# D x U term moved inside the scan loop, the gate read from a kept copy, a stack's first K projection in a PSUM slot of its own, and the last two units' residual made by TensorE

## The chip, the cores and the metric

The kernel runs on one core of one Trainium2 chip. Time is what the device takes for one execution, in microseconds (us); lower is better. A core has five engines with their own instruction streams: PE (TensorE, matrix products), DVE (VectorE), ACT (ScalarE), POOL (GpSimd) and SP, which issues transfers. They wait for one another through semaphores.

## What is computed

Input x is 2048 x 128. A stack of six layers is applied at half weight, then a Mamba block, then the same stack again, each on the layer-normalised x:

```python
x = x + 0.5 * ffn_stack(layernorm(x))
x = x + mamba(layernorm(x))
x = x + 0.5 * ffn_stack(layernorm(x))

# one of the six layers of a stack
x = attn_layer(shift_tokens(x), Wqkv, q_scale, k_scale, Wo) + x
x = ffn_layer(shift_tokens(x), g, b, W1, b1, W2, b2) + x

# attn_layer: 16 heads of 64, a window of 32 with the window before it
q, k, v = split(x @ Wqkv); q, k = l2norm(q) * qs, l2norm(k) * ks
q, k = rotated(q), rotated(k)
out = local_attention(q, k, v) @ Wo

# mamba, after projections, convolution and silu; 256 channels, 16 states
def step(s, inp):
    dA_t, dBu_t, C_t = inp
    s = dA_t * s + dBu_t
    y = einsum('bdn,bn->bd', s, C_t)
y = ys + u * D
y = y * silu(res)
return y @ out_w + x
```

## The kernel before

**Stacks.** `tensor_stack`, `scalar_stack`, `vector_stack` and `pool_stack` are the four engines' programs of a stack; `r` is 0 for the first and 1 for the second. A layer is cut into 16 tiles of 128 tokens, so a stack has N = 96 tiles, and tiles follow one another in a software pipeline: in step `s` an engine does the K projection of tile s - 19, the Q projection of tile s - 18 and so on, in an order written out by hand. PSUM is `PS` with four slots of two banks; `PSB` is the same memory by bank (slot s holds banks 2s and 2s + 1). Slot 0 takes the Q and, after it, the K projection of a tile. For each of these, ACT squares it into `SQ`, DVE multiplies it twice by tables (`q_rotate1`, `q_rotate2`, `k_rotate1`, `k_rotate2`; the second product goes to `T2`, which Q and K share), DVE sums the squares, and POOL adds the halves (`q_add_halves`, L1681, and `k_add_halves`, L1687) and scales them (`q_normalise`, L1695, and `k_normalise`, L1703) by inverse norms that ACT makes from the sums of both. POOL's order at the entry is: add the halves of Q of tile 0, `low_weights` for V (L1663), `low_input` (L1654), add the halves of K of tile 0, then scale Q. `keep_clock` is a few products whose result nobody reads. The feed-forward part works on units of 512 tokens, the last two of a stack on 256 (`UNITS - 2` and `UNITS - 1`): `low_part` (L1715, XNL = what the rounded XNH leaves), the up products, ACT's gelu, DVE's `gate`, the down products (L527), and in the last layer DVE's `half_output` (L1399 and L1401), which adds product, bias and X.

**Scan loop.** Between the stacks the Mamba block scans 2048 tokens in four chunks `h` of 512, and in each chunk 16 states `n`: 64 iterations k = 16 h + n. For each k:

- PE `spread(k + 2)` (L789) copies rows of B and C to all partitions in PSUM slot (k + 2) % 2, and `accumulate(k - 1)` (L708) adds state k - 1's product PR to the sums in banks 6 and 7.
- DVE `drive(k + 1)` multiplies DU by B (L1603 for half of the channels; L1599 for all of them when (k + 1) % 4 is 3), then two scans (L1619) with `input_step` (L1562) between them at k = 8 and 24.
- ACT `decay` (L1208, two per k), `evacuate(k + 1)` (L1194: B and C to SBUF) and `keep_state` (L1202).
- POOL `drive(k + 1)` (L1798, the other half of the channels, not when (k + 1) % 4 is 3) and `read_out(k)` (L1806: PR = state times C).

PE's stream holds `spread(k + 2)` behind `accumulate(k - 2)`, and `accumulate(k - 2)` waits for `read_out(k - 2)`. At n = 0 `accumulate` starts the sums with D times u (L706, matrix `DG`). When a chunk's 16 states are in, DVE's `gate_out` (L1639) reads the sums from PSUM and multiplies them by RES, between the two scans of k % 16 = 1. At k % 16 = 5 PE's `mamba_out` (L808 and L810) projects the gated chunk and then waits until ACT has copied the result into X (L1219, in iteration k % 16 = 6). The fourth chunk is projected inside the second stack's `q_project(1)`.

## Time and profile before

| | |
|---|---|
| Three timed runs | 3346.1, 3350.98 and 3351.53 us; median 3350.98 us |
| The profiled execution | 3348.16 us, of which its span (first to last instruction) is 3346.4 us |
| Busy | PE 3190.6 us (95%), DVE 2794.2 (84%), ACT 2504.1 (75%), POOL 2438.6 (73%) |
| First stack, Mamba block, second stack | from 0, from about 1541 and from about 1810 us of the span |
| Scan loop | from about 1584 to 1810 us |

A busy share is an average over stages. The steady stages of the stacks, in which PE is busy nearly throughout, are not touched by the change; the scan loop, the first two tiles of each stack and the last two units of each stack are.

### The profile page before, as it was taken

How to read it: one execution, taken by the hardware profiler on the slowest of the kernel's cores; microseconds unless marked ns; L12 is line 12 of the kernel's file. 1: busy time of each engine (PE TensorE's matmuls, PEld its weight loads, DVE VectorE, ACT ScalarE, POOL GpSimd, SP SyncE). 2: the span in 40 equal slices, each digit the busy share in tenths (PEclk: the TensorE clock that was granted, in tenths of full speed). 3: DMA queues.
4: the chain of work that ended last, by engine and by line, in shares of the span. 5: the costliest groups of instructions: out<-in, count | busy, mean ns of one | idle time of the engine just before them, and what ended most of it. 6: DMA issues, size and time to landing. Idle time of an engine off the chain costs nothing.

```text
span 3346.4 us, 120438 instructions
## 1 busy us (share of the span) xinstructions
PE 3190.6 (95%) x51618; PEld 2522.9 (75%) x51618; DVE 2794.2 (84%) x3204; ACT 2504.1 (75%) x3163; POOL 2438.6 (73%) x1233
## 2 busy tenths in 40 slices
PE   7999999999999999998888899999999999999999
PEld 5888888887887887874333788888888878788777
DVE  7888888888888888877897888888888888888886
ACT  5777777777777777777675677777777777777776
POOL 6777777777776776763898777777768768768764
PEclk8999999999999999999999999999999999999999
DMA  3333333233233332221000332323323323323322
GB/s 113 89 76 87 75 83 88 68 90 85 67 89 84 73 83 65 71 72 60 1 0 0 86 76 69 93 68 83 91 65 88 88 69 86 91 71 80 74 64 69
DMA packets 142299, 245.22 MB, mean 73 GB/s; under 512 B 32397, under 2 KB 34638, under 8 KB 141774
## 3 DMA queue, kind: packets, MB, share of 16 engines
q1 hardware_dynamic: 141774, 237.51, 27.9%
q8 instruction: 415, 6.80, 0.9%
q14 instruction: 110, 0.90, 0.1%
HBM read 35.01 MB, written 1.05 MB: 11 GB/s over the span
## 4 chain that ended last, share of the span: by engine, by line
PE 39%; issue 4%; DVE 3%; POOL 2%; ACT 2%; DVEq 0%; POOLq 0%; ACTq 0%
PE PS L270 7%; PE PS L390 6%; PE PS L214 4%; PE PS L410 4%; PE PS L216 3%; PE PS L215 3%; PE PS L331 3%; PE PS L527 2%; ACT ARENA L912 1%; DVE ARENA L1619 1%; PE PS L474 1%; PE PS L475 1%; PE PS L476 1%; POOL ARENA L1806 1%; PE PS L433 1%
## 5 line engine op out<-in xcount | busy, mean ns | idle before, releaser
L1695 POOL TENSOR_TENSOR ARENA<-ARENA,RN 128x1024 f32<-128x1024 f32 x192 | 365.4, 1903 | 456.5 <-ACT RN L902 456.5
L270 PE MATMUL PS<-C,ARENA 128*128 128x128 f32 x4608 | 613.5, 276 | 34.4 <-ACT ARENA L912 16.3
L1687 POOL TENSOR_TENSOR ARENA<-ARENA 128x1024 f32<-128x1024 f32 x192 | 468.4, 2439 | 233.9 <-DVE ARENA L1284 233.0
L270 PEld LDWEIGHTS PS<-C,ARENA 128*128 128x128 f32 x4608 | 512.0, 141 | 111.0 <-issue 76.6
L214 PE MATMUL PS<-WL,XH 128*128 128x512 f32 x1152 | 490.0, 425 | 14.0 <-DVE ARENA L1284 7.5
L965 ACT ACTIVATE ARENA<-PS 64x1024 f32<-64x1024 f32 x384 | 390.2, 1016 | 98.0 <-PE PS L270 94.7
L1681 POOL TENSOR_TENSOR ARENA<-ARENA 128x1024 f32<-128x1024 f32 x192 | 458.0, 2385 | 6.5 <-DVE ARENA L1269 6.4
L216 PE MATMUL PS<-WH,XH 128*128 128x512 f32 x1152 | 455.3, 395 | 0.0
L215 PE MATMUL PS<-WH,XL 128*128 128x512 f32 x1152 | 453.4, 394 | 0.0
L390 PE MATMUL PS<-ARENA 128*64 128x64 f32 x12288 | 401.1, 224 | 40.7 <-DVE ARENA L1322 24.5
L390 PEld LDWEIGHTS PS<-ARENA 128*64 128x64 f32 x12288 | 376.1, 138 | 75.8 <-issue 75.8
L1260 DVE TENSOR_TENSOR ARENA<-PS,TAB 128x1024 f32<-128x1024 f32 x192 | 235.2, 1225 | 226.3 <-ACT ARENA L881 226.3
L1709 POOL TENSOR_TENSOR ARENA<-ARENA,RI 128x1024 f32<-128x1024 f32 x192 | 365.7, 1905 | 47.5 <-DVE RI L1333 41.2
L410 PEld LDWEIGHTS PS<-ARENA 128*128 128x128 f32 x3072 | 372.2, 192 | 17.9 <-ACT ARENA L974 1.5
L1703 POOL TENSOR_TENSOR ARENA<-ARENA,RN 128x1024 f32<-128x1024 f32 x192 | 373.8, 1947 | 1.4 <-ACT RN L902 1.4
L410 PE MATMUL PS<-ARENA 128*128 128x128 f32 x3072 | 373.8, 275 | 1.1 <-ACT ARENA L974 1.1
L331 PEld LDWEIGHTS PS<-ARENA 64*32 64x32 f32 x24576 | 292.7, 105 | 69.7 <-issue 59.3
L331 PE MATMUL PS<-ARENA 64*32 64x64 f32 x24576 | 326.3, 223 | 0.2
L1314 DVE TENSOR_REDUCE MX<-PS 128x16 f32<-128x1024 f32 x192 | 234.5, 1221 | 94.6 <-PE PS L331 91.9
L974 ACT ACTIVATE ARENA<-PS 128x1024 f32<-128x1024 f32 x192 | 196.8, 1025 | 137.6 <-PE PS L390 137.6
L881 ACT ACTIVATE ARENA<-PS 128x1024 f32<-128x1024 f32 x192 | 197.2, 1027 | 100.3 <-PE PS L216 100.3
L214 PEld LDWEIGHTS PS<-WL,XH 128*128 128x128 f32 x1152 | 218.2, 189 | 70.9 <-issue 10.7
(155 smaller groups left out, 6493.9 us busy)
## 6 DMA issues: line engine op xcount, KB each, us to landing
ARENA<-ARENA SPq DMA_DIRECT2D x1152, 128.0 KB, 2.4
ARENA<-ARENA SPq DMA_DIRECT2D x768, 64.0 KB, 2.1
ARENA<-in_wqkv SPq DMA_DIRECT2D x36, 512.0 KB, 4.9
ARENA<-in_wo SPq DMA_DIRECT2D x12, 512.0 KB, 3.9
ARENA<-in_w SPq DMA_DIRECT2D x12, 341.0 KB, 4.0
ARENA<-in_w SPq DMA_DIRECT2D x12, 192.0 KB, 3.9
X<-in_xT SPq DMA_DIRECT2D x4, 256.0 KB, 5.0
out<-X SPq DMA_DIRECT2D x1, 768.0 KB, 3.5
```

What stands on the lines that cost most here:

```text
L214: nc.tensor.matmul(o, XH[:, x], WL[:, s], start=True, stop=False)
L215: nc.tensor.matmul(o, XL[:, x], WH[:, s], start=False, stop=False)
L216: last = nc.tensor.matmul(o, XH[:, x], WH[:, s], start=False, stop=True)
L270: last = nc.tensor.transpose(PS[:, slot, 128 * j:128 * j + 128], src[:, 128 * j:128 * j + 128], ident)
L331: last = nc.tensor.matmul(PS[32 * win:32 * win + 32, slot, c:c + 64], q[a:b, hp, 32 * win:32 * win + 32], kt[a:b, hp, 32 * win:32 * win + ...
L390: last = nc.tensor.matmul(out.rearrange("p (a q) -> p a q", a=2)[:, :, col:col + 32], v2[:, win, hp, :], pt[:, hp, win, :], start=True, st ...
L410: last = nc.tensor.matmul(PSB[:, bank, 0:128], w[:, 128 * j:128 * j + 128], OTS[:, 128 * j:128 * j + 128], start=j == 0, stop=j == 7)
L965: last = act.activation(blocks[a:b, :, par, :], PS[a:b, slot, :].rearrange("p (b q) -> p b q", q=32), ACT.Copy)
L1681: nc.gpsimd.tensor_tensor(QN[n % 2], QN[n % 2], T2, ALU.add).then_inc(q_add, 1)
L1687: nc.gpsimd.tensor_tensor(KN[n % 2], KN[n % 2], T2, ALU.add).then_inc(k_add, 1)
L1703: nc.gpsimd.tensor_tensor(a, a, bc(RN[:, n % 2, 16:32], 64), ALU.mult).then_inc(k_nrm, 1)
L1709: nc.gpsimd.tensor_tensor(heads(P), heads(P), bc(RI[:, n % 2, :], 64), ALU.mult).then_inc(p_nrm, 1)
```

## The change

1. **D x u.** It leaves `accumulate` at n = 0, which now starts the sums itself; after `accumulate` at n = 7 two products (new L718) add it.
2. **The gate.** ACT's new `keep_sums` copies the sums from banks 6 and 7 into Y at the end of iteration k % 16 = 1, and PE's next chunk waits for that (`m_yc`). DVE multiplies Y by RES in one instruction (new L1663, two SBUF inputs) between the scans of k % 16 = 4. The fourth chunk is gated from PSUM as before (`gate_last`).
3. **mamba_out** goes from k % 16 = 5 to 9, ACT's copy from 6 to 10.
4. **A stack's entry.** K of tile 0 is projected into slot 1 and no longer waits for `q_rotate2(0)`; its squares go to SB. Q of tile 1 waits for `q_rotate2(0)` and no longer for `k_rotate2(0)`. `carry(0)`, which writes slot 1, waits for `k_rotate2(0)`. DVE's `mamba_residual` of the second stack goes to the place ahead of `q_sums(0)`. The `keep_clock` products at K of tile 0 are gone; those at K of tile 1 are 3 where they were 4.
5. **A stack's last two units.** PE adds X with one more product per unit (`ident` times X), DVE's `half_output` is then one instruction of 128 x 256 where it was two, `low_part` of these units is DVE's, and the down products wait for each `gate` singly.

```diff
         def accumulate(pe, k):
...
                 pe.wait_ge(m_dl, 4)
-                pe.wait_ge(m_dg, 1)
             elif n == 0:
-                pe.wait_ge(m_yd, 2 * h)
+                pe.wait_ge(m_yc, 2 * h)
             for b in range(2):
-                if n == 0:
-                    nc.tensor.matmul(PSB[:, 6 + b, :], DG[:, 128 * b:128 * b + 128], UC[:, h, b, :], start=True, stop=False,
-                                     skip_group_check=True)
-                last = nc.tensor.matmul(PSB[:, 6 + b, :], ident, PR[k % 2][:, b, :], start=False, stop=n == 15,
+                last = nc.tensor.matmul(PSB[:, 6 + b, :], ident, PR[k % 2][:, b, :], start=n == 0, stop=n == 15,
                                         skip_group_check=True)
             last.then_inc(m_y, 1)
+            if n == 7:
+                pe.wait_ge(m_dg, 1)
+                for b in range(2):
+                    nc.tensor.matmul(PSB[:, 6 + b, :], DG[:, 128 * b:128 * b + 128], UC[:, h, b, :], start=False, stop=False,
+                                     skip_group_check=True)
...
-                if 0 <= h < 3 and k % 16 == 5:
+                if 0 <= h < 3 and k % 16 == 9:
                     pe.wait_ge(m_bev, k + 1)
                     mamba_out(pe, h, 2 * (k % 2))
...
+            def keep_sums(h):
+                act.wait_ge(m_y, 16 * h + 16)
+                for b in range(2):
+                    act.activation(Y[:, h, b, :], PSB[:, 6 + b, :], ACT.Copy).then_inc(m_yc, 1)
...
-                if h >= 0 and k % 16 == 1:
-                    gate_out(dve, h)
+                if h >= 0 and k % 16 == 4:
+                    dve.wait_ge(m_yc, 2 * h + 2)
+                    nc.vector.tensor_tensor(Y[:, h, :, :], Y[:, h, :, :], RES[:, h, :, :], ALU.mult).then_inc(m_yg, 1)
                 scan(k, 1)
...
                     mean_in(pe, r, 3)
-                    keep_clock(2)
+                    pe.wait_ge(i_done, 4 * r + 3)
+                    keep_clock(2, 5)
+                    pe.wait_ge(q_rot, n0 + 1)
+                    project(1, 0, 0, q_done)
+                    return
...
-                if n < 2:
-                    keep_clock(4)
+                if n == 1:
+                    keep_clock(3, 5)
...
+                if n == 0:
+                    pe.wait_ge(i_done, 4 * r + 2)
+                    project(0, 1, 1, k_done)
+                    return
...
             def down_products(u, bank):
                 q0, w, x = unit(u)
+                if u >= UNITS - 2:
+                    pe.wait_ge(x_half, 5 * r + u - 4 * (NL - 1) + 1)
+                    nc.tensor.matmul(PSB[:, bank, 0:w], ident, X[:, q0:q0 + w], start=True, stop=False)
...
+                if u >= UNITS - 2:
+                    nc.vector.tensor_scalar(X[:, q0:q0 + w], PSB[:, bank, 0:w], b2, None, ALU.add, ALU.bypass).then_inc(f_done, 1)
+                    return
```

PE's stream in the scan loop, from the first `accumulate` of the second chunk (in iteration k = 17) to `mamba_out` (k = 21), before; L706 is D x u, L708 the other products of `accumulate`, L789 `spread`, L808 and L810 `mamba_out`:

```order
L706 MATMUL PS<-ARENA 128x512
L708 MATMUL PS<-ARENA,C 128x512
L706 MATMUL PS<-ARENA 128x512
L708 MATMUL PS<-ARENA,C 128x512
L789 MATMUL PS<-WH,WL 128x512 x2
L708 MATMUL PS<-ARENA,C 128x512 x2
L789 MATMUL PS<-WH,WL 128x512 x2
L708 MATMUL PS<-ARENA,C 128x512 x2
L789 MATMUL PS<-WH,WL 128x512 x2
L708 MATMUL PS<-ARENA,C 128x512 x2
L808 MATMUL PS<-X,C 128x512
L810 MATMUL PS<-ARENA 128x512 x2
```

and in the changed kernel at k = 23 to 25, with L798 `spread`, L712 `accumulate`, L718 D x u, L817 and L819 `mamba_out`:

```order
L798 MATMUL PS<-WH,WL 128x512 x2
L712 MATMUL PS<-ARENA,C 128x512 x2
L798 MATMUL PS<-WH,WL 128x512 x2
L712 MATMUL PS<-ARENA,C 128x512 x2
L718 MATMUL PS<-ARENA 128x512 x2
L817 MATMUL PS<-X,C 128x512
L819 MATMUL PS<-ARENA 128x512 x2
L798 MATMUL PS<-WH,WL 128x512 x2
L712 MATMUL PS<-ARENA,C 128x512 x2
```

Between D x u and `mamba_out` stood the `accumulate`s of three further states; now D x u stands directly in front of `mamba_out`.

DVE's stream at the gate, before: L1619 a scan, L1639 the gate, L1599 the wide `drive`:

```order
L1619 SCALAR_TENSOR_TENSOR ARENA<-PS,ARENA 128x512
L1639 TENSOR_TENSOR ARENA<-PS,ARENA 128x512 x2
L1619 SCALAR_TENSOR_TENSOR ARENA<-PS,ARENA 128x512
L1599 TENSOR_TENSOR ARENA<-ARENA,PS 128x1024
```

and in the changed kernel, where L1648 is a scan, L1663 the gate, L1632 and L1628 `drive`:

```order
L1632 TENSOR_TENSOR ARENA<-ARENA,PS 128x512
L1648 SCALAR_TENSOR_TENSOR ARENA<-PS,ARENA 128x512
L1663 TENSOR_TENSOR ARENA<-ARENA 128x1024
L1648 SCALAR_TENSOR_TENSOR ARENA<-PS,ARENA 128x512
L1632 TENSOR_TENSOR ARENA<-ARENA,PS 128x512
L1648 SCALAR_TENSOR_TENSOR ARENA<-PS,ARENA 128x512 x2
L1628 TENSOR_TENSOR ARENA<-ARENA,PS 128x1024
```

The gate has one instruction of 1024 columns that reads no PSUM, three iterations later.

PE's stream with its waits at the second stack's entry, before: the `keep_clock` products, K of tile 0 (L214 to L216), `mamba_out`, `mean_in(3)` (L192) and Q of tile 1:

```order
L221 MATMUL PS<-X,C 128x256 x3
L214 MATMUL PS<-WL,XH 128x512 [waits s_q_rot,s_w_lok,s_x_lo]
L215 MATMUL PS<-WH,XL 128x512
L216 MATMUL PS<-WH,XH 128x512
L214 MATMUL PS<-WL,XH 128x512
L215 MATMUL PS<-WH,XL 128x512
L216 MATMUL PS<-WH,XH 128x512
L808 MATMUL PS<-X,C 128x512 [waits s_m_yd,s_m_xs]
L810 MATMUL PS<-ARENA 128x512 x2
L192 MATMUL PS<-X,C 128x512 [waits s_m_done]
L221 MATMUL PS<-X,C 128x256 x2
L214 MATMUL PS<-WL,XH 128x512 [waits s_k_rot,s_q_rot,s_w_loq,s_x_lo]
```

and in the changed kernel:

```order
L214 MATMUL PS<-WL,XH 128x512 [waits s_i_done,s_w_lok,s_x_lo]
L215 MATMUL PS<-WH,XL 128x512
L216 MATMUL PS<-WH,XH 128x512
L214 MATMUL PS<-WL,XH 128x512
L215 MATMUL PS<-WH,XL 128x512
L216 MATMUL PS<-WH,XH 128x512
L817 MATMUL PS<-X,C 128x512 [waits s_m_yg,s_m_xs]
L819 MATMUL PS<-ARENA 128x512 x2
L192 MATMUL PS<-X,C 128x512 [waits s_m_done]
L221 MATMUL PS<-X,C 128x256 [waits s_i_done]
L221 MATMUL PS<-X,C 128x256
L214 MATMUL PS<-WL,XH 128x512 [waits s_q_rot]
```

The `keep_clock` products in front of K of tile 0 are gone, and so are its wait for `q_rot` and the wait of Q of tile 1 for `k_rot`.

## Rows read from the trace of the kernel before

**Rows 1.** The page: the span, and each engine's busy time, share and instructions.

```profile
span 3346.4 us, 120438 instructions
...
PE 3190.6 (95%) x51618; PEld 2522.9 (75%) x51618; DVE 2794.2 (84%) x3204; ACT 2504.1 (75%) x3163; POOL 2438.6 (73%) x1233
```

**Rows 2.** Busy by stretch: length; PE, PEld, DVE, ACT, POOL; clock, DMA.

```profile
1645.00:1703.20 58.20, 48.01 (x108) 17.90 (x107) 53.72 (x52) 39.68 (x66) 53.18 (x29) 0.97 0.00 1
1703.20:1760.00 56.80, 47.12 (x109) 17.58 (x107) 51.87 (x51) 40.38 (x66) 52.79 (x30) 1.00 0.00 1
```

**Rows 3.** Groups by line, 1584 to 1810 us: busy, mean ns, idle before, releasers.

```profile
L1806 POOL TENSOR_TENSOR ARENA<-ARENA 128x1024 f32<-128x1024 f32 x63 | 149.9, 2390 | 19.6 <-DVE ARENA L1619 16.8 <-PE PS L708 2.8
...
L1798 POOL TENSOR_TENSOR ARENA<-ARENA 128x512 f32<-128x512 f32 x48 | 63.8, 1329 | 0.9 <-ACT ARENA L1194 0.9
```

**Rows 4.** Timeline, second chunk: start, length, engine, line, tiles, count [idle before <- releaser].

```profile
1646.22 1.29 DVE L1639 TENSOR_TENSOR ARENA<-PS,ARENA 128x512 f32<-128x512 f32 x2 [0.57 <-PE PS L708]
...
1652.56 2.37 POOL L1806 TENSOR_TENSOR ARENA<-ARENA 128x1024 f32<-128x1024 f32 x1 [1.32 <-DVE ARENA L1619]
...
1660.35 1.02 PE L808 MATMUL PS<-X,C 128*128 128x512 f32 x2
...
1664.54 1.22 DVE L1599 TENSOR_TENSOR ARENA<-ARENA,PS 128x1024 f32<-128x1024 f32 x1 [3.27 <-PE PS L789]
...
1668.26 2.36 POOL L1806 TENSOR_TENSOR ARENA<-ARENA 128x1024 f32<-128x1024 f32 x1 [2.70 <-DVE ARENA L1619]
```

**Rows 5.** Timeline around DVE's two `input_step`s (L1562).

```profile
1612.90 3.70 DVE L1562 TENSOR_TENSOR ARENA<-ARENA 128x1024 f32<-128x1024 f32 x1
...
1617.87 2.35 POOL L1806 TENSOR_TENSOR ARENA<-ARENA 128x1024 f32<-128x1024 f32 x1 [2.35 <-DVE ARENA L1619]
...
1672.76 2.49 DVE L1562 TENSOR_TENSOR ARENA<-ARENA 128x1024 f32<-128x1024 f32 x1
...
1674.10 2.28 POOL L1798 TENSOR_TENSOR ARENA<-ARENA 128x512 f32<-128x512 f32 x1
```

**Rows 6.** Timeline of the first chunk: its first accumulate, and 35 us on.

```profile
1589.14 2.07 PE L706 MATMUL PS<-ARENA 128*128 128x512 f32 x2 [2.46 <-POOL ARENA L1806]
...
1595.91 0.69 DVE L1603 TENSOR_TENSOR ARENA<-ARENA,PS 128x512 f32<-128x512 f32 x1 [2.88 <-PE PS L789]
...
1624.17 3.78 PE L708 MATMUL PS<-ARENA,C 128*128 128x512 f32 x4
...
1628.74 0.69 DVE L1603 TENSOR_TENSOR ARENA<-ARENA,PS 128x512 f32<-128x512 f32 x1 [1.40 <-PE PS L789]
```

**Rows 7.** Timeline of the second stack's entry.

```profile
1825.56 3.31 PE L221 MATMUL PS<-X,C 128*128 128x256 f32 x8 [2.51 <-DVE ARENA L1240]
...
1827.97 2.37 POOL L1681 TENSOR_TENSOR ARENA<-ARENA 128x1024 f32<-128x1024 f32 x1 [1.89 <-DVE ARENA L1269]
...
1832.25 1.27 POOL L1654 TENSOR_TENSOR XL<-ARENA,XH 128x512 fp32r<-128x512 f32 x1
...
1833.83 1.22 DVE L1284 TENSOR_TENSOR ARENA<-PS,TAB 128x1024 f32<-128x1024 f32 x1
...
1835.13 2.39 POOL L1687 TENSOR_TENSOR ARENA<-ARENA 128x1024 f32<-128x1024 f32 x1 [1.61 <-DVE ARENA L1284]
...
1838.95 1.90 POOL L1695 TENSOR_TENSOR ARENA<-ARENA,RN 128x1024 f32<-128x1024 f32 x1 [1.43 <-ACT RN L902]
```

**Rows 8.** Timeline of the first stack's entry, POOL.

```profile
30.02 2.38 POOL L1687 TENSOR_TENSOR ARENA<-ARENA 128x1024 f32<-128x1024 f32 x1
...
33.74 1.90 POOL L1695 TENSOR_TENSOR ARENA<-ARENA,RN 128x1024 f32<-128x1024 f32 x1 [1.34 <-ACT RN L902]
```

**Rows 9.** Timeline of the second stack's end.

```profile
3337.01 0.72 POOL L1715 TENSOR_TENSOR XNL<-ARENA,XNH 128x256 fp32r<-128x256 f32 x1 [5.95 <-ACT XNH L1009]
...
3340.17 2.83 PE L527 MATMUL PS<-ARENA 128*128 128x256 f32 x12
...
3343.53 0.49 DVE L1401 SCALAR_TENSOR_TENSOR X<-PS,LP,X 64x256 f32<-64x256 f32 x1
```

More of the change, by code:

```diff
@@ L175, in build @@
             "dt", "min", "ex", "sp", "dl", "du"))
-        m_bc, m_bev, m_cs, m_pr, m_dg, m_y, m_yd, m_out, m_done = (sem("m_" + n) for n in (
-            "bc", "bev", "cs", "pr", "dg", "y", "yd", "out", "done"))
+        m_bc, m_bev, m_cs, m_pr, m_dg, m_y, m_yc, m_yg, m_out, m_done = (sem("m_" + n) for n in (
+            "bc", "bev", "cs", "pr", "dg", "y", "yc", "yg", "out", "done"))
         m_da, m_db, m_sc = ([sem(f"m_{n}{b}") for b in range(2)] for n in ("da", "db", "sc"))
@@ L217, in project, with keep_clock @@
                 last.then_inc(done, 1)
-            def keep_clock(k, bank=3):
+            def keep_clock(k, bank):
                 for _ in range(k):
@@ L312, in carry @@
                     pe.wait_ge(pad_set, r + 1)
+                    pe.wait_ge(k_rot, n0 + 1)
                 s = n + 19
@@ L652, in finish_tiles @@
                 down_products(u + 1, 5)
-                for j in range(3):
-                    units(f_h[j], u + 2)
                 units(f_xm, u + 2)
@@ L878, in q_square @@
                 act.wait_ge(q_done, n0 + n + 1)
-                if n:
+                if n == 1:
+                    act.wait_ge(q_ss, n0 + 1)
+                elif n:
                     act.wait_ge(k_ss, n0 + n)
@@ L889, in k_square @@
                 act.wait_ge(k_done, n0 + n + 1)
-                act.wait_ge(q_ss, n0 + n + 1)
-                act.activation(SQ, PS[:, 0, :], ACT.Square).then_inc(k_sq, 1)
+                if n:
+                    act.wait_ge(q_ss, n0 + n + 1)
+                act.activation(SQ if n else SB, PS[:, 0 if n else 1, :], ACT.Square).then_inc(k_sq, 1)
             def inverse_norms(n):
@@ L1215, in scalar_mamba @@
                 decay(k, 0)
-                if k > 16 and k % 16 == 6:
+                if k > 16 and k % 16 == 10:
                     h = k // 16 - 1
@@ L1224, in scalar_mamba @@
                     evacuate(k + 1)
+                if k > 1 and k % 16 == 1:
+                    keep_sums(k // 16 - 1)
         def layer_tables(l, g):
@@ L1277, in k_rotate1 @@
                     dve.wait_ge(kT_done, n0 + n - 1)
-                nc.vector.tensor_tensor(halves(KN[n % 2]), halves(PS[:, 0, :]), table(n, 2), ALU.mult)
+                nc.vector.tensor_tensor(halves(KN[n % 2]), halves(PS[:, 0 if n else 1, :]), table(n, 2), ALU.mult)
             def k_rotate2(n):
@@ L1283, in k_rotate2 @@
                 dve.wait_ge(q_add, n0 + n + 1)
-                nc.vector.tensor_tensor(halves(T2), halves(PS[:, 0, :])[:, :, ::-1, :], table(n, 3),
+                nc.vector.tensor_tensor(halves(T2), halves(PS[:, 0 if n else 1, :])[:, :, ::-1, :], table(n, 3),
                                         ALU.mult).then_inc(k_rot, 1)
@@ L1292, in q_sums @@
                     return
+                if n == 0 and r == 1:
+                    mamba_residual(dve, 3, 7)
                 dve.wait_ge(q_sq, n0 + n + 1)
@@ L1391, in gate2, with low_part @@
                     gate(x // 4, 2, 2 * 1)
+            def low_part(u):
+                q0, w, x = unit(u)
+                dve.wait_ge(f_hi, c0 + u + 1)
+                nc.vector.tensor_tensor(XNL[:, x], XCT[:, x], XNH[:, x].bitcast(F32), ALU.subtract).then_inc(f_lo, 1)
             def half_output(u, bank):
@@ L1438, in vector_stack @@
             for s in range(114):
-                if s == 18 + 1 and r == 1:
-                    mamba_residual(dve, 3, 7)
                 if s == 18 + 2:
@@ L1487, in vector_stack @@
             normalise(u + 1, 4)
+            low_part(u + 1)
             if r == 0:
@@ L1493, in vector_stack @@
             normalise(u + 2, 4)
+            low_part(u + 2)
             if r == 0:
@@ L1728, in pool_stack @@
             if r == 1:
-                pool.wait_ge(m_yd, 8)
+                pool.wait_ge(m_yg, 4)
                 pool.wait_ge(m_out, 3)
@@ L1760, in pool_stack @@
             p_normalise(95)
-            low_part(UNITS - 2)
             if r == 0:
-                squares(pool, 0)
-                squares(pool, 1)
-            low_part(UNITS - 1)
-            if r == 0:
-                squares(pool, 2)
+                for c in range(3):
+                    squares(pool, c)
         def squares(pool, c):
```

26 lines of the change are left out of this document (12 added, 14 removed).

## The prediction

> **What bounds the kernel now.** I read the page first: PE is busy 95% of a span of 3346.4 us [rows 1]. The change leaves the steady stages alone, so this share says nothing of it, and I read three places instead: the scan loop, the entries and the ends of the stacks. Whatever one of them gains or loses moves everything behind it, since stack, Mamba block and stack follow one another.
>
> In the scan loop I took busy time from gate to gate. The third chunk (1703.2 to 1760) lasts 56.8 us, of which POOL is busy 52.8 and DVE 51.9; PE (47.1) and ACT (40.4) have room [rows 2]. POOL and DVE are thus both nearly full, and the loop's length is POOL's work plus the 4.0 us in which it stands still. The groups say for whom: `read_out` (L1806) waited 16.8 us for DVE's scans and once, 2.8 us, for PE [rows 3]. The timeline shows what makes DVE late, twice in a chunk: the gate (1.29 us, after 0.57 of waiting for PE), which POOL feels as 1.32, and `mamba_out`, for which DVE waits 3.27 and POOL then 2.70 [rows 4]. These two make the 4.0. `mamba_out` costs so much because the next `spread` is queued behind it and behind ACT's copy, and DVE's `drive` waits for that `spread`.
>
> **The scan loop, part by part.**
>
> *D x u out of the first accumulate.* At 1589 PE runs at the lower of its two clocks: one product of D x u takes 2.07 us, and DVE's `drive` waits 2.88 for what stands behind [rows 6]. Without the two products (some 3.4 us there, the second one meeting a rising clock) the next `spread` comes earlier by about 2.1 net of what remains cold. Take -2.1 (bounds 0 and -2.9).
>
> *The clock after k = 8.* DVE's `input_step` there holds everything, PE falls idle and comes back slow: the four passes of an `accumulate` take 3.78 us, and DVE loses 1.40 to it [rows 6]. D x u now lies in just this gap. Take -1.4 (bounds 0 and -1.4).
>
> *D x u in front of mamba_out.* A product of its shape is two passes, 1.02 us at the full clock with the next one starting a little before its end [rows 4]; the two cost 1.8. PE's stream is now `accumulate`, D x u, `mamba_out`, wait for the copy, `spread`, and DVE's wait grows from 3.27 to some 5.1. Before, D x u stood at n = 0, where DVE was at its gate. Nothing covers it now in the third and fourth chunk: +1.8 each. In the second chunk `input_step` (k = 24, 2.49 us on DVE [rows 5]) falls on the same place: before, DVE lost 1.86 + 3.27 + 2.49; now it loses 2.49 for the gate, 2.49 for `input_step`, and 5.1 less the 2.49 by which it is late itself. Both sums are 7.6, so 0. Bounds per chunk: 0, if DVE has gained enough lead since the gate, and +1.8.
>
> *The gate from SBUF.* No such gate is in the trace, but `input_step` has its shape and its kinds of operands. It took 2.49 and 3.70 us, far more than the 1.29 of the gate from PSUM. Both times POOL was working: at 1672.76 DVE got its turn when one POOL instruction ended, and POOL's next one then took 2.28 where its mean is 1.33; at 1612.90 DVE came later still, and POOL idled 2.35 afterwards [rows 3, 5]. POOL has no pause at k % 16 = 4 either. With 2.49 the gate costs DVE 2.49 where it was 1.86 with its wait, +0.6, and POOL's books (held 0.95, then idle some 0.8, where it idled 1.32) say +0.4; take +0.5 per chunk, +1.5. Bounds per chunk: -0.8 (an idle POOL, 1.1 us) and +1.8 (3.70).
>
> The Trainium skill says of this pair ("SBUF — State Buffer", "SBUF: two separate sides") that DVE with two SBUF inputs and a GpSimd op that reads SBUF exclude each other, and that the first to start has the shared ports for its whole instruction. By that rule the gate waits for one POOL instruction and the sum stands as above; by the row of 3.70, in which two POOL instructions passed, it would be 3.7 higher. The rule speaks against moving the gate to SBUF at all.
>
> *keep_sums* costs ACT two copies of 512 columns per chunk, about 1.2 us; ACT is idle 18.5 us of the second chunk [rows 2], the next `decay` is late by a microsecond that DVE spends on the second scan and on `drive`. PE's next chunk waited for DVE's gate at this point and now waits for ACT, no later. Zero; if ACT had no room, +1.2 per chunk.
>
> *The clock at the new gate.* PE is starved there about as at `input_step`. One fall costs up to 1.40 [rows 6]; I put +0.5 for the three.
>
> Loop: -2.1 - 1.4 + 0 + 1.8 + 1.8 + 1.5 + 0.5 = **+2.1**.
>
> **The entries.** In the second stack PE waits 2.51 us, runs the `keep_clock` products, and K of tile 0 comes only after Q's rotation; DVE's `k_rotate2(0)` starts at 1833.83 [rows 7]. With K in its own slot it waits for POOL's Q addition only (1827.97 + 2.37 = 1830.3, [rows 7]), 3.5 earlier. Then POOL binds: `low_weights` and `low_input` (1832.25 + 1.27 = 1833.5) stand ahead of the K addition, so that moves from 1835.13 to 1833.5, ends at 1835.9, and Q's scaling follows it directly instead of at 1838.95: **-3.1** [rows 7]. DVE's `mamba_residual`, now ahead of `q_sums(0)`, holds DVE for less than that. In the first stack POOL's K addition already follows its predecessor without a gap (30.02 to 32.40), so only the wait behind it goes: Q's scaling at 32.4 instead of 33.74 [rows 8], -1.4, and a little more for K of tile 1, which POOL's idle time leaves room for; take **-2.0**. `carry(0)` waits longer but is needed only for the first scores, several steps on. Bounds: 0, if a later wait of the ramp takes it back, and -3.5 and -2.4. Together -5.1.
>
> **The ends.** PE is the chain there: twelve passes of the down products in 2.83 us, 0.236 each, straight behind the up products, then `half_output` with 0.49 for each of its halves [rows 9]. Two products more are four passes, +0.94. One DVE instruction less gives back about 0.5. `low_part` goes from POOL's 0.72 to at most DVE's 0.49 (the nearest row of 256 columns), -0.25 [rows 9]; in the first stack PE waits for DVE's gates instead, so this gain is lost. +0.2 and +0.4, **+0.6**. Bounds 0 and +1.5.
>
> **Sum.** +2.1 - 5.1 + 0.6 = -2.4 us. The profiled execution took 3348.16 us, so 3345.8; from the median of the three timed runs, 3350.98, it is 3348.6. I predict 3347, between the two: no change that can be told, since a measurement of this kernel can tell about 0.2%, 6.7 us.
>
> **Rivals.**
>
> *The loop gains instead (22%).* DVE's lead over POOL, rebuilt between k % 16 = 4 and 9, hides D x u (0 in place of +3.6), and the gate meets POOL's pauses (-0.8 in place of +0.5, three times): -2.4 - 3.6 - 3.9 = -9.9; with half of that, about 3341. For it: PE has 9 us of room in a chunk. Against it: DVE and POOL differ by only 0.9 us of busy time per chunk [rows 2], so no lead grows in five iterations.
>
> *The entries' gain isn't kept (12%).* The ramp has its own waits, and PE's clock may fall in other places of it. Then +2.7: about 3352.
>
> *The gate lets two POOL instructions pass (8%),* as at 1612.90: +1.3 three times, about 3351.
>
> *PE's clock stays low after the new gate: slower (8%).* At that clock an `accumulate` takes 3.78 us [rows 6], and with its `spread`, some 1 us at that clock, more than the 3.55 of an iteration (56.8 / 16), so PE becomes the bound and loses 1.3 us in each of the five iterations up to D x u and `mamba_out`, and these 4 us themselves grow by up to 4: 8 per chunk and +24 in all, about 3370. It decides for slower once each fall costs over 3 us; the fall in the trace cost 1.40, and PE caught up [rows 6].
>
> The forecast itself has 50%. **Range** 3337 to 3356: down to the first rival's better half, up over the second and third with the bounds of the gate. Faster by over 0.2%: 0.26 (the first rival and the lower edge of the forecast); slower: 0.11 (the last rival and the sum of dear gate and lost entries); the same: 0.63.
>
> **What would show it.** Right: POOL's first wait of 2.8 us and DVE's 2.88 gone; full clock at 1620 to 1628; the third and fourth chunks about 2.3 us longer, with DVE waiting 5 us behind `mamba_out` and a gate of about 2.5 us; Q's scaling of tile 0 3 us closer to the end of the scan; last `half_output` at the same distance from the last up product plus a few tenths. Wrong: DVE's wait behind `mamba_out` still 3.3 (D x u hidden), gates of 1.1 or 3.7, or the ramp's later tiles at the old distance.

## The result, and the profile after

The changed kernel takes 3358.01 us (median of 17 runs, 3351.88 to 3359.57), the kernel before 3348.64 in the same comparison (17 runs, 3344.45 to 3351.74). The ratio is 1.0025, with a 95% interval of 1.0018 to 1.0031: slower by 8.4 us (6.0 to 10.4); the medians themselves lie 9.4 apart. The forecast was 3347, with a range up to 3356, and "slower" had a chance of 0.11. It was wrong.

The page of the changed kernel (engine: busy us, share, instructions; then PE's granted clock in 40 slices) answers to [rows 1]:

```profile
span 3355.8 us, 120407 instructions
PE 3199.4 (95%) x51606; PEld 2524.8 (75%) x51606; DVE 2799.7 (83%) x3201; ACT 2506.6 (75%) x3169; POOL 2437.3 (73%) x1229
...
PEclk8999999999999999998999999999999999999999
```

PE is busy 8.8 us longer with 12 products fewer on record, so some of its work ran slower. To find the place I laid both timelines over each other, taking the start of the same DVE instruction in each tile (after less before, in us; the profiled executions):

| place | after less before | so this stretch gave |
|---|---|---|
| first stack, tile 1 / tile 4 | -2.7 / -0.3 | entry: gain there, then lost in the ramp |
| first stack, last tile | -2.0 | a step of -1.5 at tile 86 |
| first scan of the loop begins | -1.8 | end of the first stack: +0.2 |
| last scan of the loop ends | +10.6 | **scan loop: +12.4** (forecast +2.1) |
| second stack, tiles 4 to 20 | +6.7 | entry: -4.0 (forecast -3.1) |
| second stack, tiles 24 to 84 | +8.4 | a step of +1.6 at tile 22 |
| second stack, last tile | +9.5 | a step of +1.2 at tile 86 |
| end of the span | +9.4 | end of the second stack: 0 |

The loop thus carries the whole loss. Its groups by line in the changed kernel (busy us, mean ns, idle time before and who ended it) answer to [rows 3]:

```profile
L1832 POOL TENSOR_TENSOR ARENA<-ARENA 128x1024 f32<-128x1024 f32 x63 | 149.3, 2381 | 28.4 <-DVE ARENA L1648 25.1 <-PE PS L712 3.0
L1632 DVE TENSOR_TENSOR ARENA<-ARENA,PS 128x512 f32<-128x512 f32 x47 | 31.4, 668 | 12.5 <-PE PS L798 12.4
L1628 DVE TENSOR_TENSOR ARENA<-ARENA,PS 128x1024 f32<-128x1024 f32 x16 | 19.5, 1222 | 13.6 <-PE PS L798 11.6 <-DVE ARENA L1648 0.5
L1663 DVE TENSOR_TENSOR ARENA<-ARENA 128x1024 f32<-128x1024 f32 x3 | 10.9, 3642 | 0.0
```

L1832 is `read_out`, L1632 and L1628 are DVE's `drive`, L1648 is the scan, L1663 the gate. POOL waits 25.1 us for DVE's scans where it waited 16.8 [rows 3]; a gate takes 3.64 us where 2.49 was forecast. The timeline at the first gate (start, us, engine, line; in brackets idle time and who ended it) shows what the gate does to the others; it answers to [rows 4]:

```profile
1651.10 2.44 POOL L1832 TENSOR_TENSOR ARENA<-ARENA 128x1024 f32<-128x1024 f32 x1
1652.20 3.65 DVE L1663 TENSOR_TENSOR ARENA<-ARENA 128x1024 f32<-128x1024 f32 x1
1653.40 1.37 POOL L1824 TENSOR_TENSOR ARENA<-ARENA 128x512 f32<-128x512 f32 x1
1655.52 0.72 PE L798 MATMUL PS<-WH,WL 64*128 64x512 f32 x2
1655.77 1.27 DVE L1648 TENSOR_TENSOR_SCAN ARENA<-PS,ARENA 128x512 f32<-128x512 f32 x1
1657.18 2.34 POOL L1832 TENSOR_TENSOR ARENA<-ARENA 128x1024 f32<-128x1024 f32 x1 [2.41 <-DVE ARENA L1648]
1659.57 3.78 PE L712 MATMUL PS<-ARENA,C 128*128 128x512 f32 x4 [3.33 <-POOL ARENA L1832]
1663.28 1.22 PE L798 MATMUL PS<-WH,WL 64*128 64x512 f32 x2
1664.43 3.78 PE L712 MATMUL PS<-ARENA,C 128*128 128x512 f32 x4
1664.54 0.69 DVE L1632 TENSOR_TENSOR ARENA<-ARENA,PS 128x512 f32<-128x512 f32 x1 [0.83 <-PE PS L798]
1669.15 0.69 DVE L1632 TENSOR_TENSOR ARENA<-ARENA,PS 128x512 f32<-128x512 f32 x1 [1.55 <-PE PS L798]
```

Read it from the top. The gate begins while POOL's `read_out` runs, and it ends 1.08 us after POOL's *next* instruction (`drive`, L1824) has ended at 1654.77: two POOL instructions passed. POOL then has nothing for 2.41 us, and PE, which needs POOL's products, stands idle for 3.33. When it goes on, an `accumulate` of four passes takes 3.78 us for 1.98, and DVE waits 0.83 and 1.55 us for the `spread` behind it. The windows of PE there (stretch, length, busy, granted clock) say why:

```profile
1650.00:1655.00 5.00, 4.34 (x12) 1.00 0.00 0
1655.00:1660.00 5.00, 1.67 (x5) 0.84 0.00 0
1660.00:1665.00 5.00, 5.00 (x7) 0.50 0.00 0
1665.00:1670.00 5.00, 5.00 (x8) 0.63 0.00 0
1670.00:1680.00 10.00, 9.31 (x23) 1.00 0.01 2
```

The granted clock of 0.50 is the lower of the two levels, 1.2 GHz. It fell at 1658.42, while PE stood idle, and rose at 1668.66. It looks the same at all three gates: 3.65, 3.63 and 3.64 us, then waits of DVE of 0.83 and 1.55, 0.83 and 1.58, 0.83 and 1.60. Of the rest of the loop, the wait of DVE behind D x u and `mamba_out`:

```profile
1673.43 1.88 PE L718 MATMUL PS<-ARENA 128*128 128x512 f32 x4
1673.47 2.36 POOL L1832 TENSOR_TENSOR ARENA<-ARENA 128x1024 f32<-128x1024 f32 x1 [0.20 <-DVE ARENA L1648]
1673.83 2.45 DVE L1648 TENSOR_TENSOR_SCAN ARENA<-PS,ARENA 128x512 f32<-128x512 f32 x2
1675.14 1.02 PE L817 MATMUL PS<-X,C 128*128 128x512 f32 x2
...
1676.00 1.88 PE L819 MATMUL PS<-ARENA 128*128 128x512 f32 x4
...
1678.57 0.73 PE L798 MATMUL PS<-WH,WL 64*128 64x512 f32 x2 [0.69 <-ACT X L1236]
...
1679.34 1.22 DVE L1628 TENSOR_TENSOR ARENA<-ARENA,PS 128x1024 f32<-128x1024 f32 x1 [3.05 <-PE PS L798]
```

It is 3.05 us here and 4.19 and 4.18 in the next two chunks, for 3.27 before [rows 4].

### The profile page after: what moved, and what is told of

It reads as the page before. It is cut to its first block and busy times, and to the rows that moved or that the text cites. A ratio compares the mean times of both kernels' runs of the same rounds, so it can differ in the third digit from the quotient of the medians.

```text
span 3355.8 us, 120407 instructions
## 1 busy us (share of the span) xinstructions
PE 3199.4 (95%) x51606; PEld 2524.8 (75%) x51606; DVE 2799.7 (83%) x3201; ACT 2506.6 (75%) x3169; POOL 2437.3 (73%) x1229
## 5 line engine op out<-in xcount | busy, mean ns | idle before, releaser
L214 PE MATMUL PS<-WL,XH 128*128 128x512 f32 x1152 | 489.8, 425 | 17.1 <-DVE ARENA L1303 6.2
L216 PE MATMUL PS<-WH,XH 128*128 128x512 f32 x1152 | 456.4, 396 | 0.0
L214 PEld LDWEIGHTS PS<-WL,XH 128*128 128x128 f32 x1152 | 218.7, 190 | 73.9 <-issue 14.2
```

Of the source, the lines that this page charges most:

```text
L214: nc.tensor.matmul(o, XH[:, x], WL[:, s], start=True, stop=False)
L216: last = nc.tensor.matmul(o, XH[:, x], WH[:, s], start=False, stop=True)
```

## The experiments

Each time stands beside runs of the kernel before on the same chip, and the ratio is to those. The kernel before took 3350.01 us beside e1, e3, e5 and e6, 3348.20 beside e2, e4, e8 and e9, and 3350.68 beside e7, e10, e11 and e12, so two medians of different groups compare to some 2 us only. The last column is the time in the profiled execution from the loop's first scan to the end of its last.

| run | what differs from the changed kernel | median us | ratio, 95% | loop us |
|---|---|---|---|---|
| (before) | | 3348.64 | 1 | 225.7 |
| (after) | | 3358.01 | 1.0025, 1.0018 to 1.0031 | 238.1 |
| e1_loop_before | loop as before | 3346.14 | 0.9993, 0.9984 to 1.0001 | 226.8 |
| e7_entries_only | loop and ends as before | 3347.70 | 0.9992, 0.9983 to 1.0001 | 224.2 |
| e3_gate_at_6 | gate at k % 16 = 6 | 3352.91 | 1.0011, 1.0002 to 1.0020 | 233.8 |
| e5_mamba_out_at_5 | `mamba_out` after 5 | 3345.06 | 0.9989, 0.9980 to 0.9998 | 225.6 |
| e6_psum_gate_dxu7_out5 | gate from PSUM, `mamba_out` after 5 | 3346.50 | 0.9993, 0.9984 to 1.0002 | 225.0 |
| e2_psum_gate_out9 | gate from PSUM | 3348.72 | 1.0001, 0.9993 to 1.0010 | 226.7 |
| e9_dxu_first | D x u in front, as before | 3349.87 | 1.0002, 0.9993 to 1.0010 | 227.7 |
| e4_filler_at_gate | surplus products on PE | 3361.83 | 1.0035, 1.0021 to 1.0048 | 241.4 |
| e12_dxu_in_hole | D x u at the gate's step | 3349.48 | 0.9999, 0.9990 to 1.0008 | 227.5 |
| e8_out5_w1_early | `mamba_out` after 5, `w1_low` earlier | 3324.26 | 0.9931, 0.9919 to 0.9944 | 224.7 |
| e10_psum_gate_w1_early | as e6, `w1_low` earlier | 3326.88 | 0.9932, 0.9919 to 0.9944 | 225.8 |
| e11_before_w1_early | kernel before, `w1_low` earlier | 3330.38 | 0.9943, 0.9930 to 0.9955 | 225.8 |

### Is it the loop?

**e1_loop_before** puts the loop back and leaves entries and ends changed.

```diff
-                if h >= 0 and k % 16 == 4:
-                    dve.wait_ge(m_yc, 2 * h + 2)
-                    nc.vector.tensor_tensor(Y[:, h, :, :], Y[:, h, :, :], RES[:, h, :, :], ALU.mult).then_inc(m_yg, 1)
+                if h >= 0 and k % 16 == 1:
+                    dve.wait_ge(m_y, 16 * h + 16)
+                    for b in range(2):
+                        last = nc.vector.tensor_tensor(Y[:, h, b, :], PSB[:, 6 + b, :], RES[:, h, b, :], ALU.mult)
+                    last.then_inc(m_yg, 1)
...
-                if 0 <= h < 3 and k % 16 == 9:
+                if 0 <= h < 3 and k % 16 == 5:
```

(`keep_sums` goes, ACT's copy moves from 10 to 6, and D x u back to n = 0.)

> Scan loop as before (gate from PSUM at k%16=1, D*u in front of a chunk's first sums, mamba_out after k%16=5), entries and ends as changed. Theory (the loss is the loop's: its last scan ended 12.4 us later against its first in the trace of after, entries and ends gained some 3 to 5): 3358.0 - 12.4 = 3345.6, range 3344 to 3348. Rival (the gains at the entries hang on the loop's new ending, or the loss is in the steady units): the time stays above the kernel before's, 3350 to 3354, and the offset in the second stack's tiles 4 to 20 is not 4 us below that at the loop's end.

3346.14, and a loop of 226.8 us for 238.1. The loss is the loop's; the rival falls.

**e7_entries_only** puts the ends back too (X added by DVE, low part made by POOL).

> Both stacks' entries as changed, loop and ends as before. Theory (the ends cost 0.2 and 0.4 by the forecast, which the traces of after bore out at about +0.4 and 0): against the run with the loop as before (3346.1) 0 to 0.6 less: 3345.5, range 3343 to 3348, not to be told from it by the median; in the trace the first scan starts 0.4 earlier against the first stack's last tile. Rival (the ends gain): 3348 to 3350.

3347.70, not to be told from e1. In the traces the stretch from the first stack's last tile to the first scan is 0.4 us (e7) and 0.2 us (e11) longer than in the kernel before, with the same end; with the new end it is 0.2 to 1.7 longer in eleven traces, 1.0 in the mean. That leaves some 0.7 for the first stack's end where 0.4 was forecast, a price that no median shows.

### Gate, place of mamba_out, D x u

**e3_gate_at_6**: one number in DVE's loop.

```diff
-                if h >= 0 and k % 16 == 4:
+                if h >= 0 and k % 16 == 6:
```

> As changed, but the gate stands at k%16=6, where POOL has one multiply to do (the read out) and not two. Theory (two POOL multiplies pass a gate that stands where POOL has two queued, and the stall of 3.33 us that this gives PE lowers its clock): each gate takes 2.5 us or less and not 3.65, PE's idle time there is 2.2 us or less, the clock stays full, and 1.15 + 0.83 + 1.57 = 3.5 us are saved per gate, 10.6 in all: 3347.5, range 3345 to 3351. Rival (the loss is D*u directly in front of mamba_out, which stays): 3354 to 3358. Rival (a gate of any length over some 2.2 us costs the clock): the gate is 2.5 us but the two accumulates after it still take 3.78: 3358 - 3.5 = 3354.5.

3352.91, between the theories. At k % 16 = 6 POOL has only its `read_out`, the gate takes 2.86, 2.84 and 2.85 us, and one POOL instruction passes. But PE still stands idle for 2.12 us at each, and behind two of the three its clock sinks, if later; the passes here come to 2.80 us:

```profile
1663.74 2.35 POOL L1832 TENSOR_TENSOR ARENA<-ARENA 128x1024 f32<-128x1024 f32 x1 [2.41 <-DVE ARENA L1648]
1666.15 2.80 PE L712 MATMUL PS<-ARENA,C 128*128 128x512 f32 x4 [2.12 <-POOL ARENA L1832]
```

Behind `mamba_out` DVE then waits 4.85, 6.93 and 4.97 us. So a gate let past one POOL instruction alone isn't the cure.

**e5_mamba_out_at_5**: the number of `mamba_out` and of ACT's copy.

```diff
-                if 0 <= h < 3 and k % 16 == 9:
+                if 0 <= h < 3 and k % 16 == 5:
...
-                if k > 16 and k % 16 == 10:
+                if k > 16 and k % 16 == 6:
```

> As changed, but mamba_out stands after k%16=5 (its copy at 6) and not 9, so that D*u is not directly in front of it. Theory (the larger part is the gate, its two POOL multiplies and the low clock after it, 3.5 us each): only the wait behind D*u and mamba_out falls away, 3 x 1.8 = 5.4 us: 3352.6, range 3350 to 3355; gates stay at 3.65. But mamba_out then falls in PE's stretch at the low clock, which may cost all of it again: 3357 to 3360. Rival (the loss is at mamba_out alone): 3346 to 3348.

3345.06, 13 us less (12 by the ratios), more than either theory gave: the gate isn't shorter, and yet nothing of the loss is left. Its timeline, in the same places as above:

```profile
1653.53 3.66 DVE L1663 TENSOR_TENSOR ARENA<-ARENA 128x1024 f32<-128x1024 f32 x1
1654.94 1.98 PE L712 MATMUL PS<-ARENA,C 128*128 128x512 f32 x4 [0.68 <-POOL ARENA L1832]
1657.34 1.10 PE L817 MATMUL PS<-X,C 128*128 128x512 f32 x2 [0.42 <-DVE ARENA L1663]
1658.27 1.88 PE L819 MATMUL PS<-ARENA 128*128 128x512 f32 x4
1658.52 2.35 POOL L1832 TENSOR_TENSOR ARENA<-ARENA 128x1024 f32<-128x1024 f32 x1 [2.41 <-DVE ARENA L1648]
1661.45 0.73 PE L798 MATMUL PS<-WH,WL 64*128 64x512 f32 x2 [1.30 <-ACT X L1236]
1662.11 1.98 PE L712 MATMUL PS<-ARENA,C 128*128 128x512 f32 x4
1662.21 1.22 DVE L1628 TENSOR_TENSOR ARENA<-ARENA,PS 128x1024 f32<-128x1024 f32 x1 [0.88 <-PE PS L798]
```

`mamba_out` (L817, L819) now does its 2.8 us of work in the very stretch in which PE stood idle. The `accumulate` behind it takes 1.98, and DVE waits 0.88 for the `spread` where it waited 3 to 4. Two losses go at once: the low clock, and `mamba_out`'s wait, which now falls into the gate's. D x u, now by itself, costs DVE a wait of 1.64 and 1.65 us in the third and fourth chunks.

**e6_psum_gate_dxu7_out5** and **e2_psum_gate_out9** take the SBUF gate away (the first part of e1's diff), and leave D x u in the middle of a chunk.

> As changed, but the gate reads PSUM at k%16=1 and mamba_out stands after k%16=5, as before; of the loop's changes only D*u in the middle of a chunk (k%16=8) is left. Theory (D*u in the middle costs nothing where nothing else of PE's stands beside it, and frees 1.8 to 2.2 us of the first sums of each chunk): 3345.6 of the loop as before, less 2.1 + 1.4 for the first chunk and up to 1.8 for each other: 3342, range 3339 to 3345. Rival (D*u costs its 1.9 us wherever it stands, since PE is the bound in steady steps): 3345 to 3348, that is the same as with the loop as before.

> As changed, but the gate reads PSUM at k%16=1 as before; D*u stays in the middle of a chunk and mamba_out after k%16=9, next behind it. With the run that had mamba_out after 5 (3346.5) this gives the price of the late place alone, without a stall at the gate and without a low clock. Theory (a wait of DVE and POOL for the spread that stands behind D*u and mamba_out in PE's queue, 3.05 to 4.2 us, of which before had 2 already): 3 x 1.8 to 3 x 2.2, thus 3351.9 to 3353.1, range 3350 to 3354. Rival (the place costs nothing if the gate does not disturb): 3346 to 3348. Rival (it carries the whole loss): 3357.

3346.50 and 3348.72. For e6 that is the rival's number, not the theory's 3342: D x u in the middle isn't told from D x u in front (3346.14). Nor is e2 the 3351.9 to 3353.1 expected: the medians lie 2.2 us apart and the intervals overlap; the loops lie 1.7 us apart in the traces, of which 0.8 arises in the first chunk, before any `mamba_out`. DVE's waits in the third chunk say why, first in e6 (behind `mamba_out`, then behind D x u), then in e2 (behind both):

```profile
1720.40 1.22 DVE L1626 TENSOR_TENSOR ARENA<-ARENA,PS 128x1024 f32<-128x1024 f32 x1 [3.26 <-PE PS L798]
1734.48 1.22 DVE L1626 TENSOR_TENSOR ARENA<-ARENA,PS 128x1024 f32<-128x1024 f32 x1 [1.64 <-PE PS L798]
```

```profile
1734.61 1.22 DVE L1626 TENSOR_TENSOR ARENA<-ARENA,PS 128x1024 f32<-128x1024 f32 x1 [4.90 <-PE PS L798]
```

Apart or together, it is 4.90 us. D x u in the middle costs about 1.6 us of waiting in each of these chunks, and its nearness to `mamba_out` adds nothing to that. Against the kernel before, whose D x u stands beside DVE's gate, e2's third and fourth chunks are 1.7 us longer each, which is the +1.8 of the prediction; its first chunk gives 1.9 back and its second 0.5. So without the SBUF gate the changed order costs next to nothing in all.

**e9_dxu_first** keeps gate and place, and takes D x u back in front.

> As changed (gate from SBUF at k%16=4, mamba_out after 9), but D*u stands in front of a chunk's first sums as before, not in the middle. Theory (D*u next to mamba_out costs about 1.8 per chunk and the first chunk's gain was 2.1 to 2.2, the rest of the loss stays with the gate): 3358 - 5.4 + 2.2 + up to 1.4 for the clock after k=8, 3355 to 3356, range 3353 to 3358. Rival (nearness of D*u and mamba_out is the main loss): 3350 or less.

3349.87. That is the rival's number, but not for its reason, since e2 against e6 shows no price of that nearness. The gate itself changed:

```profile
1655.95 2.36 POOL L1831 TENSOR_TENSOR ARENA<-ARENA 128x1024 f32<-128x1024 f32 x1
1657.50 1.88 DVE L1662 TENSOR_TENSOR ARENA<-ARENA 128x1024 f32<-128x1024 f32 x1
1658.25 2.26 POOL L1823 TENSOR_TENSOR ARENA<-ARENA 128x512 f32<-128x512 f32 x1
```

It begins later in POOL's `read_out`, 1.55 us behind its start and not 1.10, gets its turn when that ends, and takes 1.88 or 1.89 us in each chunk; now POOL's `drive` takes 2.26 for 1.3. The order changed together with a shift of half a microsecond. PE is idle for 2.11 us here, and its clock falls behind two of the three gates, for 3.4 us each and not 10.2. So this edit changed several terms at once and separates none.

### Is it the clock?

**e4_filler_at_gate** was to keep PE busy during the gate.

```diff
+                if k > 16 and k % 16 == 5:
+                    pe.wait_ge(m_bev, k + 2)
+                    for _ in range(8):
+                        one = SEL[64:128, 0:1].broadcast_to([64, 128])
+                        nc.tensor.matmul(PSB[:, 2 * ((k + 1) % 2), :], one, HR[64:128, 0:512], start=True, stop=True)
```

> As changed, with 8 extra products of TensorE in the step of each gate, in the stretch in which it stood idle for 3.33 us (their sums are overwritten; they are surplus work). Theory (of the loop's loss the low clock after the gate is a part of its own: accumulate 3.78 for 1.98, DVE waits 0.83 and 1.57 for the spread behind it): the clock stays full, both waits go, 2.4 us per gate and 7.2 in all: 3350.8, range 3348 to 3353; gates stay at 3.65. Rival (the low clock is hidden behind POOL and DVE, and the loss is mamba_out's place alone): 3356 to 3359.

3361.83, and no test of the theory. The loop is 3.3 us longer still in the trace; the medians' intervals overlap (1.0018 to 1.0031 and 1.0021 to 1.0048). The products waited for ACT, which ended only at 1660.50.

```profile
1657.16 0.73 PE L798 MATMUL PS<-WH,WL 64*128 64x512 f32 x2
1660.50 3.78 PE L815 MATMUL PS<-WH,WL 64*128 64x512 f32 x8 [2.61 <-ACT ARENA L1211]
1664.21 3.78 PE L712 MATMUL PS<-ARENA,C 128*128 128x512 f32 x4
```

PE had been idle for 2.61 us, and the surplus itself ran at the low clock (0.50 from 1660.5 to 1664.3), in front of the work.

**e12_dxu_in_hole** does it with work that is needed and waits for nothing: D x u.

```diff
+            if n == 4:
+                pe.wait_ge(m_dg, 1)
+                for b in range(2):
+                    nc.tensor.matmul(PSB[:, 6 + b, :], DG[:, 128 * b:128 * b + 128], UC[:, h, b, :], start=False, stop=False,
+                                     skip_group_check=True)
             pe.wait_ge(m_pr, k + 1)
...
-            if n == 7:
```

> As changed (gate from SBUF at k%16=4, mamba_out after 9), but D*u's four products stand ahead of PE's wait in front of the accumulate of k%16=4, in the stretch in which PE stood idle for 3.33 us during the gate. The filler of an earlier run came too late for this (it waited for ACT and ran after the clock had fallen); these wait for nothing. Theory (the loop's loss is the low clock that follows PE's idle time at the gate, and needs it): idle time 1.5 us, clock full, accumulates of 1.98, gates still 3.65; 2.4 us per gate for the clock and 0.7 for mamba_out no longer next to D*u (2.2 in three, from the runs with mamba_out after 5 and after 9): 3358.0 - 9.3 = 3348.7, range 3345 to 3351. Rival (the gate's length itself, not PE's clock, holds the loss): at most the 2.2 comes back, 3355.8 or more.

3349.48, 0.8 from the number expected. The three gates still take 3.65, 3.65 and 3.62 us, and the loop is 10.7 us shorter:

```profile
1652.82 3.65 DVE L1663 TENSOR_TENSOR ARENA<-ARENA 128x1024 f32<-128x1024 f32 x1
1656.79 1.98 PE L709 MATMUL PS<-ARENA 128*128 128x512 f32 x4
1657.80 2.35 POOL L1832 TENSOR_TENSOR ARENA<-ARENA 128x1024 f32<-128x1024 f32 x1 [2.41 <-DVE ARENA L1648]
1660.20 1.99 PE L717 MATMUL PS<-ARENA,C 128*128 128x512 f32 x4 [1.43 <-POOL ARENA L1832]
```

POOL stands still for the same 2.41 us as in the changed kernel, PE for 1.43 in place of 3.33; the granted clock is 1.00 in every window from 1640 to 1680, and the waits of 0.83 and 1.55 are gone. `accumulate` goes on 7.38 us behind the gate's start, as in the changed kernel (7.37), so PE's delay at the gate is the same and only its speed behind it differs. Of the 10.7 us, 7.2 are these waits of DVE at three gates: the clock's part. Another 2.7 go with D x u, which no longer stands in front of `mamba_out`: DVE waits 0.88, 3.26 and 3.26 us there for 3.05, 4.19 and 4.18, while `input_step` (k = 24) takes 2.48 for 1.20. The other 0.8 I can't assign. In time the run is 8.5 us faster (8.7 by the ratios), so the clock's part there is some 6, an estimate from these shares.

### The step at tile 22

In each of the changed kernels so far the second stack loses 1.4 us at tile 22. There DVE subtracts W1's high part from W1 (`w1_low`, in `ffn_residual`), reading and writing SBUF alone. In the kernel before, and then in the changed one:

```profile
2142.99 0.90 DVE L1245 TENSOR_TENSOR W1L<-ARENA,W1H 128x682 fp32r<-128x682 f32 x1
2143.13 3.00 POOL L1681 TENSOR_TENSOR ARENA<-ARENA 128x1024 f32<-128x1024 f32 x1
```

```profile
2149.59 2.38 POOL L1712 TENSOR_TENSOR ARENA<-ARENA 128x1024 f32<-128x1024 f32 x1
2149.74 2.95 DVE L1264 TENSOR_TENSOR W1L<-ARENA,W1H 128x682 fp32r<-128x682 f32 x1
```

Before, DVE was first by 0.14 us; now it is second by 0.15 and waits. In all other layers but each stack's first, this subtraction took 2.77 to 2.96 us in both kernels (1.68 in each stack's first). DVE stands idle for 1.02 us a little earlier, waiting for PE's down products, while POOL has not begun. **e8_out5_w1_early** (on e5), **e10_psum_gate_w1_early** (on e6) and **e11_before_w1_early** (on the kernel before) move it there.

```diff
+                if c % 4 == 3:
+                    w1_low(l + 1)
                 par = LP[:, l * NP:(l + 1) * NP]
                 dve.wait_ge(f_y, c0 + c + 1)
...
                 if c % 4 == 3:
-                    w1_low(l + 1)
```

> As the run with SBUF gate and mamba_out after 5 (3345.1), and DVE takes W1's low part in front of a unit's two output adds, not behind them: there DVE stood idle for 1.02 us and POOL's multiply of SBUF had not begun. In the traces this 0.90 us subtraction took 2.96 in 5 of 6 layers of each stack where it began 0.15 us after a POOL multiply, and in the second stack of before, where it began 0.14 us ahead of one, 0.90; that one case is the step of 1.4 us by which all changed kernels lose part of the entry's gain at the 22nd tile. Theory (DVE waits until POOL's multiply is done, and PE stood idle 1.30 behind it): 0.90 to 1.0 each and 1.4 us less per layer, 10 times: 3331, range 3328 to 3336. Rival (the loss is only moved, since the subtraction now delays POOL's multiply or the adds): 3343 to 3347. Rival (the step at tile 22 is something else): the offset in the second stack keeps its step.

> The run with the gate from PSUM, D*u in the middle and mamba_out after 5 (3346.5), with W1's low part ahead of the two output adds. Theory: the same gain as with the SBUF gate (3345.1 to 3324.3, 20.8): 3325.7, range 3323 to 3328.

> The kernel before with the one move of W1's low part, nothing else. Theory (the gain is independent of this change): 3348.5 - 20.8 = 3327.7; less 1.4 because one of before's ten subtractions was short already, so 3329, range 3326 to 3332. Rival (the 20.8 hangs together with the new loop and entries): over 3335.

3324.26, 3326.88 and 3330.38. The 12 subtractions of e8 take 12.1 us where the changed kernel's take 32.6, and its span is 19.4 us shorter than e5's; the step at tile 22 is gone. By the ratios the move is worth 19.4 us on e5, 20.4 on e6 and 19.1 on the kernel before: it does not need this change. The first number is 7 us better than expected: I had counted 1.4 per layer, and the offsets show 1.6 to 1.8 gained in most layers and more in a stack's last (2.4 and 3.9). There a fall of PE's clock ahead of tile 86 is gone too, which 14 of the 22 stacks without the move have and none of the six with it. e8's place, in its own timeline:

```profile
2124.65 0.87 DVE L1264 TENSOR_TENSOR W1L<-ARENA,W1H 128x682 fp32r<-128x682 f32 x1
2125.25 2.03 POOL L1727 TENSOR_TENSOR ARENA<-ARENA,RN 128x1024 f32<-128x1024 f32 x1 [6.52 <-ACT RN L914]
2125.72 0.74 DVE L1445 SCALAR_TENSOR_TENSOR ARENA<-PS,LP,ARENA 64x512 f32<-64x512 f32 x1 [0.19 <-PE PS L541]
```

The output add begins with a wait of 0.19 in place of 1.02: the subtraction fills time in which DVE waited. e8 is faster than both kernels, by 0.69% against the one before.

## Why the prediction was wrong

*Right.* The clock after k = 8 stayed at the full level, as said. It did in all eight traces with D x u behind n = 7, and fell in four of the six without (not in e1 and e11), so this term was a fall that comes in part of the executions only. The end of the second stack: +0.2 forecast, 0 measured.

*The first chunk.* -3.5 forecast in two terms, -1.6 measured at k = 17. D x u out of the first `accumulate` had gained 2.2 by the third `read_out`, the -2.1 forecast, but the loop did not keep it: PE's low clock, which before ended 9.7 us into the loop, now lasted 14.5 us, DVE waited 1.09 and 1.90 at 1592 and 1597, and by k = 4 the loop stood at +0.2. In five other traces with D x u moved the low clock lasted 13.5 to 14.2 us and the gain went in the same way. In e3, e6 and e8 it ended after 7.8, and 2.7 were kept. The clock after k = 8 then gave 1.5. Another 1.0 was luck: `input_step` took 2.67 us for 3.70, which was in no term. By k = 17 1.1 were lost again.

*The second stack's entry.* -3.1 forecast, -4.0 here, and between -2.9 and -6.0 by tile 4 in the eleven other traces with this entry. It looks right and isn't shown. The trace of e11, which has the entry of before, gains 4.6 us over the same stretch against the trace of before: that one has 17 us of low clock between the end of the scan and tile 5, e11 only 3.4. So the execution that I measured against was a slow one in this place. What can be seen of the term itself is that Q's scaling of tile 0 stands 26.6 us behind the last scan's end, for 29.0 before and 28.0 in e11: 2.4 or 1.4 us, not 3.1.

*The first stack's entry.* -2.0 forecast. Tile 1 came 2.7 earlier, and by tile 4 only 0.3 was left; over the twelve traces of kernels with this entry it is 1.0 in the mean against tile 0 (between -3.1 and +0.2), where e11 with the old entry has +0.9. The rival "the ramp takes it back" thus holds for half of the gain against the trace of before, and hardly against that of e11. What in the ramp takes it was not tried. For both entries together, -5.1 forecast, e1 and e7 give 2.3 and 2.7 us by their ratios, with intervals that just reach no change.

*The gate's price.* The step that failed first: "with 2.49 the gate costs DVE 2.49". Of the two rows of `input_step` [rows 5] I took the cheap one as the forecast and gave the dear one 8%. All three gates were of the dear kind, 3.65, 3.63 and 3.64, together +5.7 against before's gates with their waits (1.86, 1.69 and 1.66), where the sum had +1.5. The Trainium skill's rule ("SBUF — State Buffer", "SBUF: two separate sides"), by which I had supported the choice, gives a wait for one POOL instruction, the one that started first. This trace does not agree: the gate's row starts at 1652.20, POOL's `drive` at 1653.40, and yet `drive` too ends before the gate does.

*The clock at the gate.* The step that carries most of it: "+0.5 for the three". In the trace it is 0.83 + 1.55 at the first gate and as much at the others, 7.2 us, and e12 gives back all of these waits by an edit that leaves the gate as it is. I sized it from the single fall in the trace of before, 1.40 [rows 6]. After the longer gate PE is idle 3.33 us and slow through two `accumulate` and the `spread` between and behind them. The rival "PE's clock stays low after the new gate: slower" named the mechanism and gave it 8%; it asked for over 3 us per fall, and 2.4 were enough, because the dear gate came with it. I had treated as separate, with a small chance each, what is one chain: two POOL instructions pass, so POOL stands still, so PE does, so its clock falls. Of this chain e12 and e5 test the last link, idle PE and low clock, and cut the loss there; that the number of POOL instructions passed is what starts it was only read in the rows, and e3, with one passed, still had the clock fall at two gates.

*D x u in front of mamba_out.* +3.6 forecast in the last two chunks. With the gate from PSUM this is what it costs (e2: waits of 4.90 and 4.91 for 3.26, both chunks 1.7 us longer than before). In the changed kernel DVE's waits grew to 4.19 and 4.18 only, +1.9 in all; why 0.7 less each wasn't tried. The term's size was thus nearly right, its reason in part wrong, since D x u costs the same 1.6 away from `mamba_out` (e6). In the second chunk `input_step` (k = 24) took 1.20 us, 1.3 less than before, as DVE began it with POOL idle.

Adding up the loop: -1.6 (first chunk) + 5.7 + 7.2 + 1.6 (waits behind `mamba_out`: -0.2, +0.9, +0.9) - 1.3 = +11.6 of the +12.4 measured; the other 0.8 us I can't assign to a row.

*Steady units.* I had taken them as untouched. They aren't quite: with the new entry DVE's `w1_low` at tile 22 comes behind a POOL instruction (+1.4 to 1.6, in all ten changed kernels without the last edit), as it did before in nine of the other layers; that the entry is the reason isn't shown. The steps at tile 86, -1.5 in the first stack and +1.2 in the second, are a fall of PE's clock that the kernel before has in its first stack and the changed one in its second; they nearly cancel, and by the other traces the fall comes now in one stack, now in the other, now in both.
